# Probability tiles of 28 attention units turned by VectorE and an exchange, and a plain 32-bit value product

## What is computed

```python
scores = q @ k.T / sqrt(HD)                 # per batch (2) and head (16), 1024 x 1024
scores = where(causal, scores, min)
probs = softmax(scores)
out = probs @ v                             # (1024 x 1024) @ (1024 x 128)
a = concat(out over heads) @ wo + bo
```

## Time and profile before

| What | Value |
|---|---|
| runs shown: median (lowest, highest) | 1116.75 us (1116.45, 1118.06) |
| span of the profiled execution | 1115.4 us |
| PE busy | 1105.2 us (99%) |
| DVE, ACT, POOL busy | 834.9, 748.3, 638.1 us (75%, 67%, 57%) |
| PE's share of the chain that ended last | 95% |
| DMA moved | 56.54 MB |

### The profile page before, as it was taken

How to read it: one execution, slowest core, us unless ns; L and a number is a source line. 1 busy time by engine, 2 the same in 40 slices (tenths; PEclk the granted TensorE clock), 3 DMA queues, 4 the chain that set the end, 5 groups by cost and what they waited for, 6 DMA issues and landing times.

```text
span 1115.4 us, 20396 instructions
## 1 busy us (share of the span) xinstructions
PE 1105.2 (99%) x7100; PEld 1006.7 (90%) x7100; DVE 834.9 (75%) x1978; ACT 748.3 (67%) x1584; POOL 638.1 (57%) x516
## 2 busy tenths in 40 slices
PE   9999999999999999999999999999999999999997
PEld 8999899999999999999999999999999999988897
DVE  7776777777777777777777777777777777977776
ACT  5666867666666666666666666666666666688765
POOL 2217666555555555555555555555555556777676
PEclk9999999999999999999999999999999999999999
DMA  5002412121212121212121212121211212230102
GB/s 176 1 1 62 129 39 53 39 62 39 52 39 62 39 53 39 60 39 50 37 60 39 52 39 62 39 48 44 62 38 37 50 40 57 48 110 14 39 1 76
DMA packets 33285, 56.54 MB, mean 51 GB/s; under 512 B 5792, under 2 KB 10016, under 8 KB 33184
## 3 DMA queue, kind: packets, MB, share of 16 engines
q1 hardware_dynamic: 33040, 55.21, 19.9%
q10 hardware_dynamic: 144, 0.03, 0.0%
HBM read 17.47 MB, written 4.19 MB: 19 GB/s over the span
## 4 chain that ended last, share of the span: by engine, by line
PE 95%; POOL 2%; issue 1%; ACT 1%; DMA 1%; DVE 1%; SPq 0%; POOLq 0%; ACTq 0%; DVEq 0%
PE ps_m L458 58%; PE ps_s L458 23%; PE ps_t L608 12%; PE ps_m L505 1%; DMA work<-in_attn_w 0%; POOL acc L2341 0%; POOL qk_lo L2346 0%; PE ps_m L479 0%; POOL wqk_lo L2346 0%; PE ps_t L458 0%; POOL pT_lo L2354 0%; DMA work<-work 0%; POOL acc L2330 0%; PE ps_m L666 0%; PE ps_m L667 0%
## 5 line engine op out<-in xcount | busy, mean ns | idle before, releaser
L2296 POOL TENSOR_TENSOR work<-work,rope 128x512 f32<-128x512 f32 x128 | 165.5, 1293 | 222.8 <-DMA work<-work 222.7
L1784 DVE TENSOR_TENSOR pT_lo<-ps_t,pT_hi 128x512 fp32r<-128x512 f32 (+3 forms) x408 | 210.8, 551 | 32.7 <-ACT pT_hi L1201 30.2
L1201 ACT ACTIVATE pT_hi<-ps_t 128x512 fp32r<-128x512 f32 (+3 forms) x408 | 182.8, 489 | 65.3 <-PE ps_t L608 65.1
L1777 DVE CUSTOM_DVE_ANT_0 ps_s<-ps_s,causal 128x128 f32<-128x128 f32 (+7 forms) x272 | 203.5, 767 | 6.7 <-PE ps_s L458 4.1
L2300 POOL TENSOR_TENSOR work<-work 128x512 f32<-128x512 f32 x128 | 167.6, 1310 | 10.0
L2307 POOL TENSOR_TENSOR qk_lo<-work,qk_hi 128x512 fp32r<-128x512 f32 x128 | 163.0, 1293 | 17.8 <-ACT qk_hi L1158 17.8
L1152 ACT ACTIVATE work<-ps_m,bqk 128x512 f32<-128x512 f32 x128 | 88.8, 694 | 116.5 <-PE ps_m L458 116.4
L1817 DVE SCALAR_TENSOR_TENSOR acc<-ps_m,rinv,acc 128x256 f32<-128x256 f32 x272 | 118.6, 478 | 63.0 <-PE ps_m L458 61.7
L1194 ACT ACTIVATE prob_b<-ps_s,nmax 128x640 f32<-128x640 f32 (+3 forms) x136 | 130.3, 958 | 17.9 <-DVE nmax L1777 14.6
L458 PE MATMUL ps_s<-qk_hi 128*128 128x384 f32 (+5 forms) x384 | 140.6, 366 | 0.0
L1738 DVE SCALAR_TENSOR_TENSOR work<-ps_m,bqk,rope 128x512 f32<-128x512 f32 x128 | 95.5, 746 | 54.3 <-ACT work L1152 54.0
(11 more groups left out here) (235 smaller groups left out, 2822.7 us busy)
## 6 DMA issues: line engine op xcount, KB each, us to landing
work<-work SPq DMA_DIRECT2D x256, 128.0 KB, 2.3
wst<-in_head_qk SPq DMA_DIRECT2D x16, 256.0 KB, 2.9
acc<-in_x_tiles SPq DMA_DIRECT2D x8, 256.0 KB, 6.8
wo_st<-in_L_ffn_wo SPq DMA_DIRECT2D x16, 128.0 KB, 2.4
wst<-in_pair_v SPq DMA_DIRECT2D x8, 256.0 KB, 3.0
x_rows<-acc SPq DMA_DIRECT2D x4, 512.0 KB, 3.6
wst<-in_expert SPq DMA_DIRECT2D x8, 256.0 KB, 3.0
rope<-x_rows SPq DMA_DIRECT2D x4, 512.0 KB, 4.1
```

The lines of the kernel that those rows point to most:

```text
L1201: act.activation(pT_hi[:, slots, cols], t_bank(u, i, j)[:, 0:size * P].rearrange("p (j q) -> p j q", q=P), ACT.Copy).then_inc(t_hi.sem, t_ ...
L1777: dve.tensor_tensor_reduce(s, s, causal[:, T - (i + 1) * P:T], -1.0, ABOVE_ALL, ALU.add, ALU.min, accum_out=nmax[:, u % 2, i:i + 1]).then_ ...
L1784: dve.tensor_tensor(pT_lo[:, slots, cols], t_bank(u, i, j)[:, 0:size * P].rearrange("p (j q) -> p j q", q=P), pT_hi[:, slots, cols].bitcas ...
L2296: pool.tensor_tensor(qs[:, x % 2, :], qs[:, x % 2, :], sin_t[:, c * CH:(c + 1) * CH], ALU.mult).then_inc(sin_done.sem, sin_done.up(u, x))
```

## The change

In the 28 units 3 to 30 (`TURNED`) PE makes no transposes. DVE `turn_probs(u, i)` turns each tile of probabilities as blocks of 32 x 32 with one instruction. Its input view reads every fourth word: `probs(i).rearrange("p (j k g) -> p j g k", g=4, k=Q4)`. It writes runs of 32 words. For half c = 0 the destination is `shared_ln` (the space of `rows` and `hf` in one piece), for c = 1 it is `pT`. After the fourth tile of a half SP `exchange(u, c)` issues four DMAs, from 32 partitions each, which bring each quarter of the queries to all 128 partitions: 256 KB each for c = 0 into `early_pT`, 512 KB each for c = 1 into `we2`. So an exchange moves 1 MB or 2 MB, 3 MB for a unit. `exchange` waits for the turns and for the value product of the unit before.

The value product is one plain 32-bit product for each key tile instead of three fp32r products, in all 34 units. The splits of probabilities and values are gone: ACT copies the values (`copy_values`), and in the units that still use PE's transposes ACT copies the turned block (`copy_p`). DVE has no `low_p` and no `low_values`. In the 28 units the second half's product is done one unit later: `far_outputs` (key tiles 0 to 3, in two pieces) and `near_outputs` (4 to 7) stand in `head(u + 1)`. The banks taken in turn are four there, since `ps_t` is free. The order of all engines in `head(u)` is written anew. PE's new order is q part 0, scores 4, q part 1, scores 5, far piece 0, scores 6, far piece 1, scores 7, near, q parts 2 and 3, early, two `out_project` of the unit before, scores 0 to 3 of the next unit, and values and `out_project` in turn.

```diff
+TURNED = range(3, LAST - 2)
+Q4 = 32
...
-        v_hi = sb("v_hi", [P, 2, NT, D], F32R)
-        v_lo = sb("v_lo", [P, 2, NT, D], F32R)
-        pT_hi = sb("pT_hi", [P, NT, CH], F32R)
-        pT_lo = sb("pT_lo", [P, NT, CH], F32R)
+        values = sb("values", [P, 2, NT, D])
+        pT = sb("pT", [P, NT, CH])
+        we2 = sb("we2", [P, 2, EXPERTS * CH], F32R)
+        early_pT = sb("early_pT", [P, TC, CH])
...
+        turned = (shared_ln[:, :], pT[:, :, :].rearrange("p j n -> p (j n)"))
+        moved = tuple(x.rearrange("p j n -> p (j n)") for x in (early_pT[:, :, :], we2[:, :, :].bitcast(F32)))
...
-                    last = product(out[:, off:CH], (v_hi[:, s, j, vals], v_lo[:, s, j, vals]),
-                                   (pT_hi[:, slot, off:CH], pT_lo[:, slot, off:CH]), j == 0, j == tiles - 1)
+                    last = pe.matmul(out[:, off:CH], values[:, s, j, vals], pT[:, slot, off:CH], start=j == 0,
+                                     stop=j == tiles - 1)
...
+            def block_product(u, c, j, last):
+                s, h, off = values_of(u) % 2, half_of(u), max(0, j - TC * c) * Q4
+                out = by_quarter(m_bank("pv", u, c))[:, :, off:P]
+                probs_ = moved[c].rearrange("p (g j n) -> p g j n", g=4, n=P)[:, :, j, off:P]
+                return pe.matmul(out, values[:, s, j, h * HD:(h + 1) * HD], probs_, start=j == 0, stop=last)
+
+            def far_outputs(u, k):
+                if k == 0:
+                    take_bank("pv", u, 1)
+                    pe.wait_ge(exchanged[1].sem, exchanged[1].at(u))
+                for j in (2 * k, 2 * k + 1):
+                    block_product(u, 1, j, False)
...
-            def low_p(u, i):
...
+            def turn_probs(u, i):
+                c = i // TC
+                dve.wait_ge(exp_done.sem, exp_done.at(u, i))
...
+                elif i % TC == 0:
+                    dve.wait_ge(exchanged[c].sem, exchanged[c].at(u - 1))
+                to = turned[c].rearrange("p (g j i q) -> p j i g q", g=4, i=TC, q=Q4)[:, 0:i + 1, i % TC, :, :]
+                blocks = probs(i).rearrange("p (j k g) -> p j g k", g=4, k=Q4)
+                dve.transpose(out=to, in_=blocks).then_inc(turn_done.sem, turn_done.up(u, i))
...
+            def exchange(u, c):
+                sp.wait_ge(turn_done.sem, turn_done.at(u, TC * c + TC - 1))
+                sp.wait_ge(pv_mm.sem, pv_mm.at(u - 1, c))
+                source, to = (x.rearrange("p (g n) -> p g n", g=4) for x in (turned[c], moved[c]))
+                for g in range(4):
+                    sp.dma_start(to[:, g, :], source[g * Q4:(g + 1) * Q4, :, :]).then_inc(exchanged[c].sem, 16)
...
             def ends():
+                far_outputs(TURNED[-1], 0)
+                far_outputs(TURNED[-1], 1)
+                near_outputs(TURNED[-1])
                 scores(LAST - 2, 4)
```

More of the change, by code:

```diff
@@ L1017, in _ @@
             start()
-            for u in range(3, LAST - 2):
+            recent[:0] = [2, 3]
+            for u in TURNED:
                 head(u)
+            recent[:] = [n for n in recent if n < 2]
             ends()
@@ L1346, in start @@
                 high_o(2, 0)
[L1347 removed]
+                copy_p(2, 4)
                 ln_affine(3, 0)
@@ L1582, in _ @@
         def _(dve):
+            for j in range(1, TC):
+                ins = dve.memset(pT[:, TC + j, 0:j * P], 0.0)
+            ins.then_inc(pT_cleared, 1)
             def link(ins, links):
@@ L1934, in start @@
                 row_max(0, 5)
-                low_values(0, 3)
                 accumulate(0, 0, 1)
-                low_p(0, 4)
                 ln_apply(1, 1)
@@ new lines, in head @@
+                if r == 3:
+                    low_qk_weights(p + 1, 1)
+                turn_probs(u, 4)
+                rotate(n, 0)
+                row_max(u, 6)
+                rotate(n, 1)
+                turn_probs(u, 5)
+                row_max(u, 7)
+                invert(u, 0)
+                turn_probs(u, 6)
+                rotate(n, 2)
+                if by_blocks(u - 1):
+                    low_o(u - 1, 1)
+                turn_probs(u, 7)
+                accumulate(u - 1, 1, 0)
@@ new lines, in head @@
+                rotate(n, 3)
+                row_max(n, 0)
+                row_max(n, 1)
+                low_o(u, 0)
+                row_max(n, 2)
+                accumulate(u - 1, 1, 1)
+                row_max(n, 3)
+                accumulate(u, 0, 0)
+                if by_blocks(n):
+                    turn_probs(n, 0)
+                    turn_probs(n, 1)
+                    turn_probs(n, 2)
+                    turn_probs(n, 3)
+                accumulate(u, 0, 1)
+                invert(u, 1)
```

472 lines of the change are left out of this document (208 added, 264 removed).

## The result

The changed kernel takes 1206.1 us (median of 4 runs, 1204.8 to 1212.7), the kernel before 1116.9: a ratio of 1.081, 95% interval [1.078, 1.084]. The forecast was 1071 us, the range 1052 to 1135. The change costs 89 us where a gain of 46 was expected, and the time lies outside the range. The profiled execution is the slowest of the four (1212.7 us), so sums against its span of 1210.9 us are some 6 us above the median.

The account below looks back on a forecast made before the run. PE was taken to bound the kernel, busy 1105.2 of 1115.4 us. 28 units falling from 28.26 to 26.0 us (0.35 us stall included) save 63.3, 17.9 is added elsewhere: 1070.0 by span, 1071 by median, range 1052 to 1135.

Parts of the forecast that it names:

- PE's part of a unit: In the 28 units: transposes going saves 4.2 us, the plain product costs 1.5 more; unit 28.26 to 25.65 us.
- The turn: DVE's block turns, reading every fourth word: 1.6 ns a column, 8.6 us a unit, 1.8 us for tile 7.
- the two comparisons of the earlier trace: Small gating comparisons writing with a step of four words: 1.6 ns a column on L1842, 2.3 on L1845.
- The exchange: Second half's move between partitions: 2.1 MB at the swap's 211 GB/s, 9.9 us, plus 1.7 fixed, 11.6 us.
- The threshold of 13.7 us: Exchange length above which the change is a loss: unit over 27.6 us, or 2.1 MB at under 175 GB/s.
- The page on the ports: Skill page cited: partitions 0 to 31 and 0 to 63 on the same eight ports, 189 and 196 GB/s.
- half the rate: Case of half as many source partitions halving the exchange's rate: exchange 21.6 us, unit 35.5, kernel 1336 us.
- The loop beside the exchange: From `far_outputs` through scores, near product, q part 2, bias, `rotate`, `low_o` and turn of tile 7: 13.7 us.
- my rival: The exchange ends last in the 28 units: a unit is 13.9 us plus the exchange's latency; chance 0.20.
- Outside the 28 units: Plain products in the other units, 6.4 and 6.0 us, and 5.5 in `ends()`: 17.9 us more.
- The sum: Whole kernel: 28 x (28.26 - 26.0) = 63.3 us less, 17.9 more, 1115.4 to 1070.0 by the span.
- The exchange comes last: Rival: PE waits for the second half's exchange in the 28 units, kernel over 1119 us; chance 0.20.

Follow-up runs that it names:

- the plain product alone: The kernel before, with its order and PE's transposes, but one plain 32-bit value product instead of three fp32r products: 1158.5 us, 1.037.
- an exchange of 12.4 us: The changed kernel with each transfer of both exchanges reading two blocks from 64 partitions instead of four from 32: 1101.5 us, 0.985 to the kernel before.
- one of 14.0: The changed kernel with an exchange's four transfers issued in the order of source quarters 0, 2, 1, 3: 1157.0 us, 1.036 to the kernel before.
- the late order: The changed kernel with PE computing scores 4 to 7 and all q parts ahead of the far, near and early products: 1088.9 us, 0.975 to the kernel before.

## Why the prediction was wrong, point by point

- **PE's part of a unit: right.** Where nothing waits, a unit is 25.47 us; predicted 25.65, from the earlier trace rows. The far (2 x 1.72), near and early products (2.16 each) sum to 7.76 us; I took 8.1, with a lower bound of 7.8. Calls of 512 columns cost 0.43 us a MATMUL. That the product is a loss is confirmed by the plain product alone (+41 us); since a unit without waits still fell from 28.26 to 25.47 us, the gain is, by difference, that of the transposes.
- **The turn: right in kind, short in size.** Predicted 1.6 ns a column and 1.8 us for tile 7 from the earlier trace rows, measured 2.05 us. From 896 to 1,024 columns it grows by 2.0 ns a column, from 128 (0.40 us) to 1,024 by 1.84, between the two comparisons of the earlier trace rows. All eight turns take 9.7 us a unit, where 8.6 were predicted. My reason for the lower figure, that L1845 also repeats an input, was no reason: L1842 repeats one too. DVE stayed off the critical path except in the loop: 0.25 us a unit. The Trainium skill's page "Vector Engine (DVE) Microarchitecture Reference", § Measured stream behaviour on trn2, gives 1.7 to 2.5 ns a column without adjacent pairs; the trace agrees, at its lower end.
- **The exchange: the step that failed.** "A swap reads 64 partitions and an exchange DMA 32, so I go by the swap: 2.1 MB / 211 = 9.9 us." It measured 15.1 us, 139 GB/s with everything included, where 11.6 were predicted. The 211 was worked out as a rate by a share of 0.18, and I held it for more likely too low. In the sum's own terms (9.9 for the bytes, 1.7 fixed) the same transfers took 12.4 us from 64 partitions, so the sum was 0.8 us short even for a source like the swap's. The other 2.7 us are the step from 64 partitions to 32, which I had left at nothing. The place was right: I wrote that a long exchange makes the change a loss. The threshold of 13.7 us was somewhat high, since it left out the clock: an exchange of 12.4 us still gained 15 us and one of 14.0 lost 40, so by a straight line between these two runs it lies at an estimated 12.9 us.
- **The page on the ports.** My paragraph let it stand against half the rate. Half the rate over the whole exchange did stay out, and in the middle of an exchange 32 and 64 partitions were not far apart (196 and 216 GB/s). But the estimate that the exchange would remain under 13.7 us was wrong: 15.1.
- **The loop beside the exchange.** Predicted 13.7 us; in the chain 601.59 - 586.23 = 15.4, and 15.6 in the median of the units. Of the 1.7 us more in the chain, 1.5 are the far product, 3.38 + 1.72 = 5.1 instead of 3.6, since its first part ran at the half clock, and 0.2 the turn. I had priced no wait by its clock. So even my rival was short: its 13.9 + 15.1 = 29.0 us for a unit would give 28 x 0.74 = 21 us above 1115.4, and 17.9 more, 1154 us; the kernel takes 1206.
- **Outside the 28 units: about right.** 1210.9 - 28 x 30.95 = 344.3 us, against 1115.4 - 791.3 = 324.1 before: 20.2 more; predicted 17.9, with a wait of 4.5 us in `ends()` that measured 7.2.
- **The sum.** The unit was missed by 30.95 - 26.0 = 4.95 us, 28 times: 139 us of the 141 between 1070.0 and 1210.9.
- **The chances.** "The exchange comes last" had 0.20, on one row of a nearly idle queue. With DMAs from 32 partitions in no row, and two cycles tied within 0.1 us (25.6 and 25.65), the chance was too low: 2 us upward in the loop were enough for a loss by my own sum, and waits cost clock besides.

## What to carry to other kernels

A transfer between partitions has to be priced by how many partitions it reads and writes; a rate from transfers of 64 partitions was nearly right for 64 and wrong for 32. When a computed loop ties with an engine's own work, reorder first: the late order won 117 us over the changed kernel with the same transfers. And a long wait of PE is to be priced with the products behind it at half clock; with waits of at most 2.4 us in the units (64 source partitions) the mean granted clock stayed at 0.991, against 0.953.

## What the runs showed of the hardware

- Moves inside SBUF, 2.1 MB in rows of 4 KB, over the whole exchange: some 270 GB/s from 128 to 128 partitions (405 in a window inside it), 169 from 64, 139 from 32, and 101 from 128 into 32.
- DMA engines read as full (share 0.96 to 1.08) at 121, 211 and 405 GB/s alike. The share doesn't tell whether the bytes move fast.
- SP takes 7.6 us to issue four DMAs of 512 KB from 32 partitions (median 7.8), 5.8 from 64 and 3.2 from 128, and what stands behind them on SP is issued late too. It is not the transfer's length alone: from 128 into 32 partitions, the slowest of all, the four issues take 3.4 us.
- A block turn costs 1.23 us for 1,024 columns of adjacent words, 2.05 us with a step of four.
- The granted clock fell to 0.5 toward the end of 4.9 us in which PE had no work, and PE's first products of 512 columns behind it ran at that level for some 3 us.
